# A state-space scan on one core: drive products on 64x64 tiles, softplus terms added by TensorE, every other chunk's gating on VectorE

## What is computed

```python
delta = softplus(dt @ Wdt.T + dt_bias)
def step(state, xs):
    d_t, B_t, C_t, u_t = xs
    dA = exp(d_t[..., None] * A)
    state = dA * state + (d_t * u_t)[..., None] * B_t[:, None, :]
    y_t = einsum('bdn,bn->bd', state, C_t)
    return state, y_t
_, ys = scan(step, init, xs)
y = (swapaxes(ys, 0, 1) + u * D_param) * silu(gate)
return y @ W_out.T
```

## Time and profile before

| | |
|---|---|
| median of the timed runs | 4029.22 us |
| profiled execution, device time | 4035.27 us |
| its span in the profile | 4033.5 us |
| TensorE matmuls busy | 3869.3 us (96%) |
| VectorE busy | 2690.4 us (67%) |
| GpSimd busy | 2212.4 us (55%) |
| ScalarE busy | 2057.1 us (51%) |

### The profile page before, as it was taken

How to read it: one execution, slowest core, us unless ns; L and a number is a source line. 1 busy time by engine, 2 the same in 40 slices (tenths; PEclk the granted TensorE clock), 3 DMA queues, 4 the chain that set the end, 5 groups by cost and what they waited for, 6 DMA issues and landing times.

```text
span 4033.5 us, 59248 instructions
## 1 busy us (share of the span) xinstructions
PE 3869.3 (96%) x22816; PEld 2547.3 (63%) x22816; DVE 2690.4 (67%) x2934; ACT 2057.1 (51%) x3012; POOL 2212.4 (55%) x960
## 2 busy tenths in 40 slices
PE   4899999999999999999999999999999999999999
PEld 1568777444777777544577877744477877744466
DVE  6855572999446573699835555499935557289953
ACT  7842344777332344777523233677723234387732
POOL 0023433999534343799733334599943343389962
PEclk7999999999999999999999999999999999999999
DMA  4242234000322224200132223400032223410022
GB/s 114 79 145 80 86 104 159 23 16 16 118 93 86 79 84 137 98 16 16 61 114 95 79 77 117 153 13 16 26 125 94 84 84 105 160 31 16 16 89 73
DMA packets 97131, 320.23 MB, mean 79 GB/s; under 512 B 12400, under 2 KB 16752, under 8 KB 92400
## 3 DMA queue, kind: packets, MB, share of 16 engines
q1 hardware_dynamic: 80752, 275.70, 21.4%
q10 hardware_dynamic: 16128, 41.03, 3.0%
HBM read 272.51 MB, written 44.17 MB: 79 GB/s over the span
## 4 chain that ended last, share of the span: by engine, by line
PE 36%; issue 32%; DVE 20%; POOL 9%; ACT 2%; POOLq 0%; ACTq 0%; DVEq 0%
PE psg L985 22%; DVE sb_wst L1798 17%; POOL sb_wl L537 9%; PE psx L1220 5%; PE psg L1241 3%; PE psx L1293 1%; PE psg L1271 1%; DVE psg L1771 1%; DVE psg L1770 1%; PE psg L1369 1%; PE psg L1278 1%; ACT sb_yh L898 1%; PE psx L1002 0%; PE psg L1260 0%; PE psg L1195 0%
## 5 line engine op out<-in xcount | busy, mean ns | idle before, releaser
L537 POOL TENSOR_TENSOR sb_wl<-sb_raw,sb_wh 128x1024 fp32r<-128x1024 f32 x388 | 955.1, 2465 | 1740.9 <-ACT sb_wh L654 1740.6
L1798 DVE TENSOR_TENSOR_SCAN sb_wst<-sb_dA,psx 128x1024 f32<-128x1024 f32 x512 | 1130.0, 2268 | 12.3 <-PE psx L1220 10.4
L654 ACT ACTIVATE sb_wh<-sb_raw 128x1024 fp32r<-128x1024 f32 x388 | 407.4, 1053 | 544.1 <-PE psg L985 268.8
L796 ACT ACTIVATE sb_dA<-sb_dlt,sb_a_sb 128x504 f32<-128x504 f32 x1024 | 647.3, 705 | 56.0 <-DVE sb_wst L1798 53.8
L1220 PEld LDWEIGHTS psx<-sb_dgB,sb_duT 64*128 64x128 f32 x4096 | 359.9, 188 | 447.5 <-DVE sb_wst L1798 309.1
L1220 PE MATMUL psx<-sb_dgB,sb_duT 64*128 64x256 f32 x4096 | 587.5, 406 | 35.3 <-DVE sb_wst L1798 33.3
L1241 PE MATMUL psg<-sb_wst,sb_cst 64*64 64x512 f32 x4096 | 605.7, 617 | 0.9 <-ACT sb_twin L787 0.9
L572 POOL TENSOR_TENSOR sb_wst<-sb_wst,sb_cb_lo 128x1024 f32<-128x1024 f32 x256 | 600.3, 2370 | 5.0 <-DVE sb_wst L1798 5.0
L572 POOL TENSOR_TENSOR sb_wst<-sb_wst,sb_cb_hi 128x1024 f32<-128x1024 f32 x248 | 577.6, 2365 | 24.7 <-DVE sb_wst L1798 24.7
L985 PE MATMUL psg<-sb_xh,sb_wh 128*128 128x512 f32 x2080 | 535.6, 400 | 16.1 <-POOL sb_wl L537 7.1
L985 PE MATMUL psg<-sb_xh,sb_wl 128*128 128x512 f32 x2080 | 516.7, 390 | 0.0
(11 more groups left out here) (278 smaller groups left out, 4946.9 us busy)
## 6 DMA issues: line engine op xcount, KB each, us to landing
sb_raw<-in_w SPq DMA_DIRECT2D x360, 512.0 KB, 3.6
sb_raw<-w_ffn_dequantized SPq DMA_DIRECT2D x32, 512.0 KB, 3.3
gates<-sb_gt ACTq DMA_DIRECT2D x64, 256.0 KB, 2.6
sb_gin<-gates SPq DMA_DIRECT2D x64, 256.0 KB, 2.6
h_after_tok<-sb_h SPq DMA_DIRECT2D x4, 2048.0 KB, 8.7
sb_cb_lo<-c_rows ACTq DMA_DIRECT2D x8, 1024.0 KB, 6.2
sb_cb_hi<-c_rows ACTq DMA_DIRECT2D x8, 1024.0 KB, 7.5
sb_h<-h_after_tok SPq DMA_DIRECT2D x4, 2048.0 KB, 8.5
```

Source lines behind the costliest of these rows:

```text
L537: pool.tensor_tensor(rest(b, i0), raw[:, i0 % RAW, :, :], high(b, i0).bitcast(F32), ALU.subtract).then_inc(s_wl, 1)
L654: A(high(b, i0), raw[:, i0 % RAW, :, :], ACT.Copy).then_inc(s_wh, 1)
L796: ins_ = A(dA[:, (m * NQ + k) % RING, :, n, 1:S], dlt[:, m % 2, :].rearrange("p (b s) -> p b s", b=NB)[:, :, 1:S], ACT.Exp, scale=a_sb[:, ...
L1798: v.tensor_tensor_scan(wst[:, x, 4 * j:4 * j + 4, :, :].rearrange("p b n s -> p (b n s)"), dA[:, x, 4 * j:4 * j + 4, :, :].rearrange("p b ...
```

## The change

1. `drives`: each 64x128 stationary part is split into two of 64x64 (c = 0, 1), which write the lower and the upper 64 partitions of the same bank. The number of matmuls doubles, from 4 to 8 per step in the text and from 8 to 16 in the profile, where each float32 matmul is two.
2. Softplus: ScalarE's fourth operation gives -(1 + exp) instead of 1 + exp, its logarithm takes scale -1. VectorE keeps one operation in `soft_sum` (the rounding rest) and one in `drive_sum` (the product with u). The two additions that VectorE loses are made by TensorE, `logarithm(m)`: two matmuls of the 128x128 identity with `dlt` (relu) and with `spt` (logarithm), 512 columns each, accumulated into bank 2. In the scan stage it stands in TensorE's stream after the sums of iteration g == 2, in the gate stage after the strips 10 and 14. `drive_sum` waits for it.
3. Gating: the even chunks keep the old way (ScalarE copy, GpSimd product). For the odd ones VectorE multiplies straight out of bank 2, after step 6 of the next chunk; ScalarE's copy is dropped. The semaphore of y is split in two for this, and the waits of SyncE (loads of `gin`), of `delta` and of the output stage follow. VectorE's wait for the other gatings before chunk 15's is dropped.
4. In the gate stage `drive_sum` comes one strip later for both chunks, and ScalarE makes `decay(0, 1)` before it copies delta of chunk 1.

```diff
@@ SyncE
-                        sp.wait_ge(s_y, b * DC + m - 1 + CR_Y)
+                        if m >= 2 and m % 2 == 0:
+                            sp.wait_ge(s_y, b * (DC // 2) + m // 2)
+                        if m >= 2 and m % 2 == 1:
+                            sp.wait_ge(s_yo, b * (DC // 2) + m // 2)
@@ GpSimd
-                            if g == 1 and m >= 2:
+                            if g == 1 and m >= 2 and m % 2 == 0:
                                 gated(m - 2)
@@ ScalarE
-                        A(spt[:, 1, :], x, ACT.Identity, bias=C("one")).then_inc(s_sp1, 1)
+                        A(spt[:, 1, :], x, ACT.Identity, bias=C("minus_one"), scale=-1.0).then_inc(s_sp1, 1)
                         act.wait_ge(s_sp1, b * DC + m + 1)
-                        A(spt[:, 0, :], spt[:, 1, :], ACT.Ln).then_inc(s_sp2, 1)
+                        A(spt[:, 0, :], spt[:, 1, :], ACT.Ln, scale=-1.0).then_inc(s_sp2, 1)
...
+                            decay(0, 1)
                             settled(1)
-                            decay(0, 1)
...
-                            if m >= 1:
+                            if m % 2 == 1:
                                 summed(m - 1)
@@ TensorE
                         if m >= 3:
-                            pe.wait_ge(s_yc, b * (DC - 1) + m - 2)
+                            if m % 2 == 1:
+                                pe.wait_ge(s_yc, b * (DC // 2) + (m - 3) // 2 + 1)
+                            else:
+                                pe.wait_ge(s_yo, b * (DC // 2) + (m - 4) // 2 + 1)
...
+                    def logarithm(m):
+
+                        pe.wait_ge(s_own["sp"], b * DC + m + 1)
+                        pe.matmul(psg[:, 2, :], C("ident"), dlt[:, m % 2, :], start=False, stop=False, skip_group_check=True)
+                        pe.wait_ge(s_sp2, b * DC + m + 1)
+                        pe.matmul(psg[:, 2, :], C("ident"), spt[:, 0, :], start=False, stop=True,
+                                  skip_group_check=True).then_inc(s_ln, 1)
...
                         for e in range(2):
                             i = 2 * j + e
-                            for r in range(2):
-                                r0 = 64 * r
-                                ins_ = mm(psx[:, 2 * j + r, :].rearrange("p (a t e) -> p a t e", a=8, e=2)[:, :, :, e],
-                                          duT[r0:r0 + 64, m % 2, i * P:(i + 1) * P],
-                                          dgB[r0:r0 + 64, i, k, :, :, :], start=True, stop=True)
+                            for c in range(2):
+                                for r in range(2):
+                                    r0 = 64 * r
+                                    ins_ = mm(psx[64 * c:64 * c + 64, 2 * j + r, :].rearrange("p (a t e) -> p a t e", a=8, e=2)[:, :, :, e],
+                                              duT[r0:r0 + 64, m % 2, i * P + 64 * c:i * P + 64 * c + 64],
+                                              dgB[r0:r0 + 64, i, k, :, :, :], start=True, stop=True)
...
+                        if m == 10:
+                            logarithm(0)
...
+                        if m == 14:
+                            logarithm(1)
...
                             sums_due(m * G + g - 3)
+                            if g == 2 and 1 <= m < DC - 1:
+                                logarithm(m + 1)
@@ VectorE
                         v.wait_ge(s_sp1, b * DC + m + 1)
-                        own.link(stt(x, spt[:, 1, :], 1.0, x, ALU.subtract, ALU.subtract))
-                        own.link(tt(x, dlt[:, m % 2, :], x, ALU.subtract))
+                        stt(x, spt[:, 1, :], 1.0, x, ALU.add, ALU.add).then_inc(s_own["sp"], 1)
...
-                        v.wait_ge(s_sp2, b * DC + m + 1)
+                        v.wait_ge(s_ln, b * DC + m + 1)
                         if m >= 1:
                             v.wait_ge(s_tr, b * DC + m)
-                        own.link(tt(x, spt[:, 0, :], x, ALU.add))
                         tt(du[:, :], x, u[:, m, :], ALU.mult).then_inc(s_dlt, 1)
...
                                 drive_sum(m + 1)
+                            if g == 6 and m >= 2 and m % 2 == 0:
+                                gated(m - 1)
...
-                    v.wait_ge(s_y, b * DC + DC - 1 + CR_Y)
                     gated(DC - 1)
```

More of the change, by code:

```diff
@@ L105, in constants @@
     put("one", np.ones((P, 1)))
+    put("minus_one", np.full((P, 1), -1.0))
     put("tie", np.tile(np.tile(np.arange(NEXP, 0, -1), T // P), (P, 1)))
@@ L351, in tower @@
         s_zr = sem("s_zr")
+        s_ln = sem("s_ln")
+        s_yo = sem("s_yo")
         s_yh, s_yl = sem("s_yh"), sem("s_yl")
@@ L560, in gated @@
                     def gated(m):
-                        pool.wait_ge(s_yc, b * (DC - 1) + m + 1)
+                        pool.wait_ge(s_yc, b * (DC // 2) + m // 2 + 1)
                         pool.wait_ge(s_gin[m % 2], 16 * (b * (DC // 2) + m // 2 + 1))
@@ L896, in y_high @@
                         for m in ms:
-                            act.wait_ge(s_y, b * DC + m + 1 + CR_Y)
+                            act.wait_ge((s_y, s_yo)[m % 2], b * (DC // 2) + m // 2 + 1)
                             A(yh[:, m, :], u[:, m, :], ACT.Copy).then_inc(s_yh, 1)
@@ L1345, in _ @@
                     out_highs(0, 3, YH_ORDER[5:8])
-                    pe.wait_ge(s_yc, b * (DC - 1) + DC - 1)
+                    pe.wait_ge(s_yc, b * (DC // 2) + DC // 2)
                     finals(DC - 1, False)
@@ L1435, in _ @@
             v.sem_inc(s_scan, CR_SCAN)
-            v.sem_inc(s_y, CR_Y)
             v.wait_ge(s_mode, 80)
@@ L1767, in soft_sum @@
                         x = psg[:, 2, :]
-                        own = Own(v, s_own["sp"], b * 3 * DC + m * 3)
                         v.wait_ge(s_sp1, b * DC + m + 1)
-                        own.link(stt(x, spt[:, 1, :], 1.0, x, ALU.subtract, ALU.subtract))
-                        own.link(tt(x, dlt[:, m % 2, :], x, ALU.subtract))
+                        stt(x, spt[:, 1, :], 1.0, x, ALU.add, ALU.add).then_inc(s_own["sp"], 1)
                     def drive_sum(m):
                         x = psg[:, 2, :]
-                        own = Own(v, s_own["sp"], b * 3 * DC + m * 3 + 2)
-                        v.wait_ge(s_sp2, b * DC + m + 1)
+                        v.wait_ge(s_ln, b * DC + m + 1)
                         if m >= 1:
                             v.wait_ge(s_tr, b * DC + m)
-                        own.link(tt(x, spt[:, 0, :], x, ALU.add))
                         tt(du[:, :], x, u[:, m, :], ALU.mult).then_inc(s_dlt, 1)
@@ L1786, in gated @@
                         v.wait_ge(s_gin[m % 2], 16 * (b * (DC // 2) + m // 2 + 1))
-                        tt(u[:, m, :], psg[:, 2, :], gin[:, m % 2, :], ALU.mult).then_inc(s_y, 1)
+                        tt(u[:, m, :], psg[:, 2, :], gin[:, m % 2, :], ALU.mult).then_inc(s_yo, 1)
                     def scan(m, g):
```

## The result

The changed kernel takes 4007.06 us (median, 4005.09 to 4010.18) against 4029.1 us: ratio 0.9945, 95% interval 0.9929 to 0.9961, so 22 us or 0.55% faster. 4008.4 had been predicted. Its profiled execution took 4005.5 us, span 4003.6 us. First the page's busy times, to be held against the earlier trace rows: TensorE has 4352 more matmuls and is busy 27.5 us less.

The account below looks back on a forecast made before the run. VectorE was taken to bound the kernel, and TensorE's stretch from scan 1 to scan 6 the changed one. Per block -5.8 - 1.8 + 2.4 = -5.2, four times -20.8, gives 4008.4 us; range 3975 to 4050.

Parts of the forecast that it names:

- The bound: Scan stage: VectorE sets the pace; GpSimd and TensorE stand 0.4 us behind per chunk.
- VectorE's terms: VectorE per scan chunk: alone it would need 18.81 us in an odd and 19.46 in an even chunk.
- The drives: TensorE, scan steps: 64x64 drives take 0.86 us, sums 0.86, no change between; -0.36 us per step, 2.9 per chunk.
- rival (c): TensorE, scan stage: the drives do not pack and take 1.07 us; slower, 4060 us; chance 0.18.
- The logarithm: TensorE, scan stage: two identity products cost 2.0 us per chunk; `drive_sum` does not wait for them.
- Rival (b): TensorE's logarithm in the scan stage costs 0.37 us more, eating all gain: within 0.2%, 4029 us; chance 0.17.
- The stretch up to scan 6: TensorE from scan 1 on: scan 6 starts at 10.77 after a 0.69 us wait; mean period 19.82, -0.41.
- Rival (a): TensorE's stretch hides in scan chunks and GpSimd sets 19.16 us: in all -57.6 us, 3972; chance 0.15.
- In sum TensorE has 1 us less per chunk: TensorE, scan stage: 1 us less work per chunk than before, and it catches up behind scan 6.
- Periods and edges: Scan stage: fourteen periods give -5.8 us per block; scan waits in chunks 0, 1 and 15 should go, -1.8.
- Gate stage: Before the scan: first logarithm paid in full, second fills 1.02 us of a wait, leaving 0.69; +2.4 us per block.
- The sum and the median: Whole kernel: -5.2 us per block, four times -20.8; put on the median 4029.2 this gives 4008.4 us.

Follow-up runs that it names:

- the finals' move: Changed kernel with finals(m - 1) one iteration later in TensorE's stream (g == 5 instead of 4), all work kept: 3976.8 us, ratio 0.9865.
- the kernel with finals at 6: Changed kernel with finals at iteration 5 in even and 6 in odd chunks, gate-stage additions back on VectorE: 3970.6 us, ratio 0.9851.

## Why the prediction was right, step by step

- **The bound.** VectorE bound before, GpSimd and TensorE 0.4 behind: right. Taking time from TensorE alone left 20.22; giving VectorE 0.60 more lengthened every second chunk by all of it.
- **VectorE's terms.** Right within 0.15: it needs 18.74 in an odd chunk (19.56 - 0.82), or 18.67 by starts (an even chunk without a wait takes 19.27, 0.60 of it the gating); 18.81 was worked out. The operations that stayed occupy 0.58 and 0.59 by starts (1786.77 to 1787.36, 1791.73 to 1792.31); the gating costs 0.60, for which I took 0.65 from a row of the same shape.
- **The drives.** 0.86 and no extra between them and the sums: right. By the Trainium skill ("TensorE: Matmul & The Clock Gate", the part on packing small matmuls) loads overlap matmuls only for another row group; worked out for this kernel, that was the 1.07 of rival (c), 4060 us. This case's trace does not agree: 16 loads and 16 matmuls in two row groups follow the sums at 0.86. Nor do the about 60 cycles for each matmul of the Trainium skill ("TensorEngine Tiling (Array Packing)", Instruction Overhead) show here: doubling their number took no time. Rival (c) fell in every kernel that had the new drives.
- **The logarithm.** 1.91 by starts, 2.0 predicted with its changes; no wait ahead of the product with u, as the step said. Rival (b) fell.
- **The stretch up to scan 6.** Drives 6 start 9.66 after the zero (9.62 predicted) and scan 6 10.82 (10.77). The wait is the term that was mis-sized, 0.82 for 0.69, because VectorE was ready 0.07 earlier and the drives came 0.05 later. Period 19.56 and 20.16 for 19.49 and 20.14. That the stretch was the cause is shown by the finals' move. Rival (a), no stretch, would have been 3972 us; the kernel with the move reached 3977.
- **"In sum TensorE has 1 us less per chunk" and catches up.** For the changed kernel this held, with less room than I said: its gaps are 0.20 to 0.23 once per chunk. The load is at most 19.24 (the kernel with finals at 6 shows no idle time), where 19.8 - 2.9 + 2.0 = 18.9 was meant: the step gave the equal tiles 2.9 per chunk, and 21.55 less 19.24 puts it at 2.3 or more. It did no harm here, but that I asked only for the stretch and not for the load was the miss in the kernel without the drives' part.
- **Periods and edges.** Fourteen periods gave -5.2 for -5.8 (19.86 on average for 19.82), the edges -2.1 for -1.8: chunk 0 takes 17.45 for about 19.0, chunk 15 17.55 for 18.14. Together the scan stage came out at -7.4 for -7.6. That the edges fit is in part luck. The step put the gain in chunk 0 on shorter drives, and the row with 64x128 drives at full clock takes the same 17.45: the waits in chunk 0 came with a granted clock of 0.82. Chunk 1 kept an excess of about 0.55 over its period (20.12 for 19.56; 20.78 for 20.23 before), which the step had going away. Only chunk 15 went as the step said.
- **Gate stage.** +2.35 for +2.4. The first logarithm is paid in full; the second costs 0.60, as it fills most of a wait (from the last group of strip 14 to the second of strip 15 5.39 us, 1634.87 to 1640.26, against 4.79 before). Its removal gave back 9.6 us where 9.4 were expected.
- **The sum and the median.** -20.2 for -20.8 in the profiled executions, up to 6 of it the clock in chunk 0. I had put the difference on the median, which fell by 22.0. Why the profiled execution of before lay 6 us above its median is not shown; of its 9.7 us in stages that the change leaves alone, about 4 lie where its clock was lower. So the mechanism in the steady chunks and in the gate stage is shown, and that the total came within 1.4 us of the forecast is closer than the terms deserve.

## What to carry to other kernels

Where three engines are within 2% of each other, cost two things for the loaded one: the stretch between two hand-overs, and its whole load per period. The first set the changed kernel and a move by one iteration took it away (30 us); the second set the kernel without the drives' part, and by the same count no order can help there (no run tried one). The worth of a part depends on what bounds beside it: the drives' shape gave 11 us alone and 100 beside the logarithm; the gatings on VectorE cost some 13 us alone, gained nothing in the changed kernel, and gained 41 us once TensorE's stretch was gone. And before a gain at a stage's edge is put down to a change, compare the granted clock of the two windows.

## What the runs showed of the hardware that I had not expected

- TensorE changes between 64x128 and 64x64 tiles at a price: 2.08 us for a pair of drives and sums that takes 1.73 with equal tiles, and at least 2.3 us of load per chunk of eight pairs. It is the change and not the 64x128 tile: two of the old drives one behind the other take 2.00 us (line 1220 at 1652.25), two of the new 1.96 (line 1238 at 1643.98).
- After 2.2 us without work TensorE's granted clock fell in some blocks and not in others. In block 1 the sums behind such a gap took 1.02 by starts. In block 3 the same sums took 1.67 and `finals` 1.91 (1.01 by starts in the ordinary stream), and the window of this stretch has a mean granted clock of 0.69: part of it ran at the lower of the two levels, 1.2 for 2.4 GHz. What decided between the blocks was not tried.
